# Later cycles of a coupling net computed from two products of the given state, with GpSimd's share of the work moved into the attention

## The reference, cut to what matters

```python
x = x + layernorm(attention(layernorm(x)))   # 16 heads of 8, on the left 128 features, then Wo to 256
x = x + layernorm(ffn(layernorm(x)))

def ffn(x):                                  # x: (batch, 1024, 256)
    gf = global_net(x.mean(axis=1))          # 256 -> 128 -> 64 -> 1, gelu, gelu, sigmoid
    out = x
    for _ in range(3):                       # three cycles
        tf = coupling_net(out)               # 256 -> 256 -> 128 -> 64 -> 1, three gelus, sigmoid
        coupling = 0.1 + adaptive_range * (0.7 * gf + 0.3 * tf - 0.5) * 2.0
        out = out + coupling * twist(out)
    return out

def twist(x):
    o_r, o_i, p_r, p_i = split(x, 4)
    return concatenate([p_r, -p_i, -o_r, o_i])
```

## Time and profile before

| what | value |
|---|---|
| median of 3 runs | 3441.96 us (3440.69 to 3444.75) |
| the profiled execution | 3440.79 us, span 3439.0 us |
| mean granted TensorE clock | 0.983 |
| PE / DVE / ACT / POOL busy, of the span | 96% / 86% / 84% / 28% |
| first exponential of batch 0, batch 1 | 74.4 us, 288.9 us |
| last exponentials end, span ends | 3299.4 us, 3439.0 us |

### The profile page before, as it was taken

How to read it: one execution, slowest core, us unless ns; L and a number is a source line. 1 busy time by engine, 2 the same in 40 slices (tenths; PEclk the granted TensorE clock), 3 DMA queues, 4 the chain that set the end, 5 groups by cost and what they waited for, 6 DMA issues and landing times.

```text
span 3439.0 us, 55797 instructions
## 1 busy us (share of the span) xinstructions
PE 3287.0 (96%) x19328; PEld 933.0 (27%) x19328; DVE 2964.2 (86%) x5517; ACT 2898.3 (84%) x3806; POOL 976.4 (28%) x1382
## 2 busy tenths in 40 slices
PE   6989999999999999999999999999999999999987
PEld 2222232322223232232322223232232322223222
DVE  7998989888898988989898898988989898898932
ACT  3868879798897979889798897979889798896964
POOL 5012060421406033060422406033060422404024
PEclk7998999999999999999999999999999999999998
DMA  3111111121112111111121112111111121111001
GB/s 89 26 40 43 43 38 32 43 50 42 51 32 59 33 49 44 47 45 32 42 51 42 51 32 61 32 48 45 47 45 31 43 50 42 39 32 48 7 22 37
DMA packets 97337, 144.71 MB, mean 42 GB/s; under 512 B 49312, under 2 KB 59936, under 8 KB 89248
## 3 DMA queue, kind: packets, MB, share of 16 engines
q1 hardware_dynamic: 93360, 123.83, 13.6%
q0 software_dynamic: 3696, 17.31, 2.7%
HBM read 34.61 MB, written 32.51 MB: 20 GB/s over the span
## 4 chain that ended last, share of the span: by engine, by line
PE 70%; DVE 14%; ACT 9%; issue 4%; SPq 2%; POOL 1%; DMA 1%; DVEq 0%; POOLq 0%
PE heads_ps L503 24%; PE ring_ps L470 14%; PE scoresT_ps L488 11%; DVE max_parts L949 10%; PE scoresT_ps L590 7%; ACT p_sb L700 4%; PE scoresT_ps L595 3%; DVE stats L960 2%; PE scoresT_ps L598 2%; ACT headsT L709 1%; PE scoresT_ps L601 1%; PE ring_ps L532 1%; SPq L337 1%; PE scoresT_ps L518 1%; PE heads_ps L470 1%
## 5 line engine op out<-in xcount | busy, mean ns | idle before, releaser
L949 DVE TENSOR_REDUCE max_parts<-ring_ps 128x1 f32<-128x512 f32 x3741 | 2367.9, 684 | 230.1 <-PE ring_ps L470 171.0
L700 ACT ACTIVATE p_sb<-scoresT_ps 128x1024 f32<-128x1024 f32 x2048 | 1970.9, 1025 | 82.7 <-PE scoresT_ps L488 59.1
L470 PE MATMUL ring_ps<-k_rows,q_rows 48*128 48x512 bf16 x3741 | 1079.3, 385 | 22.8 <-DVE max_parts L949 13.4
L503 PE MATMUL heads_ps<-p_sb,v_sb 128*9 128x512 f32 x8192 | 1072.5, 596 | 17.9 <-ACT headsT L709 11.9
L488 PE MATMUL scoresT_ps<-q_rows,k_rows 51*128 51x512 bf16 x4096 | 1020.6, 383 | 14.9 <-ACT p_sb L700 7.5
L470 PEld LDWEIGHTS ring_ps<-k_rows,q_rows 48*128 48x128 bf16 x3741 | 262.9, 94 | 1321.2 <-DVE max_parts L949 1210.7
L1210 POOL CAST max_wide<-max_all 128x16 bf16<-128x16 f32 x128 | 25.1, 196 | 1755.6 <-DVE max_all L955 1755.6
L590 PE MATMUL scoresT_ps<-state,w 128*128 128x512 f32 x736 | 366.6, 621 | 5.3 <-DVE state L1013 3.9
L488 PEld LDWEIGHTS scoresT_ps<-q_rows,k_rows 51*128 51x128 bf16 x4096 | 207.3, 93 | 243.3 <-ACT p_sb L700 219.9
L811 ACT ACTIVATE p_sb<-scoresT_ps,b 128x512 f32<-128x512 f32 x180 | 123.5, 686 | 167.5 <-PE scoresT_ps L590 166.6
L503 PEld LDWEIGHTS heads_ps<-p_sb,v_sb 128*9 128x9 f32 x8192 | 124.6, 89 | 288.7 <-issue 277.4
(11 more groups left out here) (206 smaller groups left out, 2767.4 us busy)
## 6 DMA issues: line engine op xcount, KB each, us to landing
q_rows<-parts SPq DMA_DIRECT2D x744, 32.0 KB
k_rows<-parts SPq DMA_DIRECT2D x744, 32.0 KB
x_sb<-in_x SPq DMA_DIRECT2D x16, 1024.0 KB, 4.9
x_in<-in_x SPq DMA_DIRECT2D x15, 1024.0 KB, 5.2
out<-x_sb SPq DMA_DIRECT2D x15, 1024.0 KB, 3.9
out<-x_in POOLq DMA_DIRECT2D x15, 1024.0 KB, 7.8
q_rows<-max_rows SPq DMA_DIRECT2D x512, 3.0 KB
feat_h<-headsT SPq DMA_DIRECT2D x512, 16.0 KB
```

The lines of the kernel that those rows point to most:

```text
L470: e.matmul(ring_bank(max_taken, u + 1), q_rows[rows, slot, pair, h * BANK + qb * P:h * BANK + (qb + 1) * P], k_rows[rows, slot, pair, kh * ...
L503: m = e.matmul(heads_ps[32 * j:32 * j + DH + 1, :], v_sb[:, b % 2, kb, 4 * (group % NG) + j, 0:DH + 1], p_sb[:, n % 2, j, :], start=(kb == ...
L700: e.activation(p_sb[:, n % 2, 2 * two:2 * two + 2, :].rearrange("p h n -> p (h n)"), scoresT_ps[:, 2 * two * BANK:(2 * two + 2) * BANK], A ...
L949: e.tensor_reduce(max_parts[:, gi % 2, kh, col:col + 1], bank_of(max_taken, u + 1), AX.X, ALU.max).then_inc(max_taken, 1)
```

## The change

Three things are done, and the beats are laid out anew (26 instead of 30 per coupling).

First, layer 1 of cycles 1 and 2 has no matmul. Cycle 0 computes u (layer 1) and v ("layer 5", the same weights with signs, on the swapped halves of the state), ACT copies both into `headsT`, which is free by then, and `mix` makes the input of the gelu from them: m = 0 on DVE, m = 1 on GpSimd, two instructions each per half c. Before the third cycle's mix, `fold` makes v - c0 u, four instructions per half c on GpSimd (in the last batch on DVE). The gelu of these reads `feat_h` and `sums_h` in SBUF.

Second, the state itself no longer stands in the way of the cycles. GpSimd makes it from the couplings of all three cycles in `spin`, six times four or more instructions per batch, in steps 5 to 20 of the next attention. The sign of the twist goes into the turned state and the weights once.

Third, the split of queries and keys is GpSimd's alone, three instructions for each of four pieces, in steps 0 to 3 of the attention; SP lays the rows from step 8 on. The first norm of batch b+2 goes from ACT to DVE (`first_norm`).

```diff
-LAYERS = ((1, 0, 0), (1, 0, 1), (2, 0, 0), (1, 1, 0), (3, 0, 0), (1, 1, 1), (4, 0, 0), (2, 1, 0), (3, 1, 0), (4, 1, 0))
-CYCLE = len(LAYERS)
-BEATS = 3 * CYCLE
+LAYERS = ((0, 1, 0, 0), (0, 1, 0, 1), (0, 5, 0, 0), (0, 2, 0, 0), (0, 5, 0, 1), (0, 3, 0, 0), (0, 1, 1, 0),
+          (0, 4, 0, 0), (0, 1, 1, 1), (0, 2, 1, 0), (0, 5, 1, 0), (0, 3, 1, 0), (0, 5, 1, 1), (0, 4, 1, 0),
+          (1, 2, 0, 0), (1, 3, 0, 0), (1, 2, 1, 0), (1, 4, 0, 0), (1, 3, 1, 0), (1, 4, 1, 0),
+          (2, 2, 0, 0), (2, 3, 0, 0), (2, 2, 1, 0), (2, 4, 0, 0), (2, 3, 1, 0), (2, 4, 1, 0))
+BEATS = len(LAYERS)
...
-BEAT_UNITS = (4, 1, 2, 1, 2, 1, 2, 2, 1, 1,
-              2, 3, 2, 3, 3, 2, 2, 4, 2, 1,
-              2, 1, 2, 3, 4, 2, 2, 2, 3, 1)
+BEAT_UNITS = (5, 6, 0, 0, 4, 0, 1, 2, 1, 3, 1, 3, 5,
+              5, 0, 2, 0, 3, 4, 3, 0, 4, 4, 2, 3, 3)
...
-STATS0, ROOT0, NORM0, TURN_X = (0, 1, 2, 3), 3, (5, 6, 7, 8), (8, 9)
-PROJECT_QK, SPLIT, PROJECT_V = (17, 18, 23, 24), (20, 21, 26, 27), (22, 29)
-BACK, STATS3, ROOT3, NORM3, ADD_OUT = (8, 9, 10, 11), (10, 11, 12, 13), 14, (16, 17, 20, 24), 26
-INVERT, DIVIDE, WO, STATS1, ROOT1 = 2, (4, 5), (5, 5, 6, 6), (6, 6, 7, 7), 7
-NORM1, ADD1, STATS2, ROOT2 = (10, 11, 12, 13), (11, 12, 13, 15), (14, 16, 17, 18), 19
-NORM2, STATE = (21, 22, 23, 24), (26, 27, 28, 29)
-GLOBAL = (0, 3, 5)
-TWIST0, UPDATE0, TWIST1, UPDATE1 = 6, 7, 9, 10
+SPLIT, SPIN = (0, 1, 2, 3), (5, 8, 11, 14, 17, 20)
+FIRST_ROW = 8
+STATS0, ROOT0, NORM0, TURN_X = (0, 0, 0, 0, 0, 2, 2, 2), 6, (4, 6, 7, 7, 7, 9, 9, 9), (7, 10)
+PROJECT_QK, PROJECT_V = (13, 14, 19, 20), (19, 23)
+BACK, STATS3, ROOT3, NORM3, ADD_OUT = (8, 9, 10, 11), (10, 10, 11, 12), 12, (13, 13, 16, 21), 25
+INVERT, DIVIDE, WO, STATS1, ROOT1 = 3, (7, 7), (7, 7, 7, 7), (7, 7, 8, 8), 8
+NORM1, ADD1, STATS2, ROOT2 = (9, 10, 11, 11), (9, 10, 11, 12), (14, 15, 16, 16), 16
+NORM2, STATE = (18, 19, 21, 21), (22, 23, 24, 25)
+GLOBAL = (1, 5, 6)
+MIX1, GELU1, FOLD, MIX2, GELU2 = (8, 13), (10, 14), (9, 15), (17, 18), (19, 20)
...
+END_SPIN, LAST_SPIN = (12, 15, 20, 20, 27, 28), (9, 15, 18, 19)
...
@@ sync_program @@
-                        for at in range(3 * n // 2, 3 * (n + 1) // 2):
+                        first, last = (96 * max(0, k - FIRST_ROW) // (STEPS - FIRST_ROW) for k in (n, n + 1))
+                        for at in range(first, last):
                             lay_row(b + 1, at)
@@ tensor_program, coupling @@
                 if layer == 1:
...
+                    e.wait_ge(state_ready, 4 * b + 2 * c + 2)
+                    e.matmul(ps, w1[:, 0, cols], state[:, b % 2, 0, half], start=True, stop=False)
+                    o = e.matmul(ps, w1[:, 1, cols], state[:, b % 2, 1, half], start=False, stop=True)
+                if layer == 5:
+                    e.matmul(ps, w1[:, 0, cols], state[:, b % 2, 1, half], start=True, stop=False)
+                    o = e.matmul(ps, w1_minus[:, cols], state[:, b % 2, 0, half], start=False, stop=True)
+                if layer == 2:
+                    e.wait_ge(activated, gelu_end(b, cycle, c, 1))
...
@@ scalar_program @@
-            def split_mid(b, i, h):
...
+                if layer in (1, 5):
+                    if m == 0:
+                        e.wait_ge(heads_laid[c], LAID * min(N, b + 2))
+                    e.activation((u_of if layer == 1 else v_of)(c, m), ps, ACT.Copy).then_inc(hid_done, 1)
...
+            def later_layer_1(b, j):
+                for cycle, places in ((1, LAST_GELU1), (2, LAST_GELU2)) if b == N - 1 else ((1, GELU1), (2, GELU2)):
+                    for c in range(2):
+                        if j == places[c]:
+                            for m in range(2):
+                                e.wait_ge(mixed[m], mix_end(b, cycle, c))
+                                e.activation(hidden[:, 0, 2 * c + m, :], turned(c, m), ACT.Gelu,
+                                             bias=b1[:, m:m + 1]).then_inc(activated, 1)
@@ vector_program @@
-            def twist(b, cycle, c):
...
-            def update(b, cycle, c):
...
+            def mix(b, cycle, c, m=0):
+                n, u, v, to = mix_end(b, cycle, c), u_of(c, m), v_of(c, m), turned(c, m)
+                by = couple_of(cycle - 1, c)
+                e.wait_ge(coupled, couple_end(b, cycle - 1, c))
+                if cycle == 1:
+                    e.wait_ge(wo_done, 4 * min(N, b + 2))
+                    e.tensor_tensor(to, by, v, ALU.mult).then_inc(mix_begun[m], 1)
+                    e.wait_ge(mix_begun[m], n)
+                    e.tensor_tensor(to, to, u, ALU.add).then_inc(mixed[m], 1)
+                else:
+                    e.wait_ge(folded, 2 * b + c + 1)
+                    e.tensor_tensor(v, by, v, ALU.mult).then_inc(mix_begun[m], 1)
+                    e.wait_ge(mix_begun[m], n)
+                    e.tensor_tensor(to, to, v, ALU.add).then_inc(mixed[m], 1)
...
+            def first_norm(b, j):
...
@@ gpsimd_program @@
+            def split(b, i, h):
+                cols, rest = slice(h * BANK, (h + 1) * BANK), proj_sb[i][h]
+                e.wait_ge(qk_evac, 4 * b + 2 * i + h + 1)
+                finished(e.tensor_tensor(rest, rest, parts[:, i, 0, cols], ALU.subtract))
+                finished(e.tensor_copy(parts[:, i, 1, cols], rest))
+                e.tensor_tensor(parts[:, i, 2, cols], rest, parts[:, i, 1, cols], ALU.subtract).then_inc(low_done, 1)
...
+            def fold(b, c):
+                by = couple_of(0, c)
+                for m in range(2):
+                    e.wait_ge(mixed[m], mix_end(b, 1, c))
+                e.tensor_tensor(u_of(c, 0), by, u_of(c, 0), ALU.mult)
+                finished(e.tensor_tensor(u_of(c, 1), by, u_of(c, 1), ALU.mult))
+                e.tensor_tensor(v_of(c, 0), v_of(c, 0), u_of(c, 0), ALU.subtract)
+                e.tensor_tensor(v_of(c, 1), v_of(c, 1), u_of(c, 1), ALU.subtract).then_inc(folded, 1)
...
+            def spin(b, cycle, c):
+                cols, by = slice(c * BANK, (c + 1) * BANK), couple_of(cycle, c)
+                real, other = state[:, b % 2, 0, cols], state[:, b % 2, 1, cols]
+                if cycle < 2:
+                    e.wait_ge(coupled, couple_end(b, cycle, c))
+                else:
+                    e.wait_ge(hid_done, end_of(b, 2, 4, c))
+                    finished(e.tensor_scalar(by, by, ar_token[:, 0:1], shift[:, 0:1], ALU.mult, ALU.add))
+                e.tensor_tensor(proj_sb[0][0], by, other, ALU.mult)
+                finished(e.tensor_tensor(proj_sb[0][1], by, real, ALU.mult))
+                e.tensor_tensor(real, real, proj_sb[0][0], ALU.add)
+                last = e.tensor_tensor(other, other, proj_sb[0][1], ALU.subtract)
...
```

More of the change, by code:

```diff
@@ new lines, in mixes @@
+            def mixes(b, j):
+                for cycle, places in mix_places(b):
+                    for c in range(2):
+                        if j == places[c]:
+                            mix(b, cycle, c)
+                        if j == LAST_FOLD[c] and cycle == 1 and b == N - 1:
+                            fold(b, c)
+            def fold(b, c):
+                by = couple_of(0, c)
+                for m in range(2):
+                    e.wait_ge(mixed[m], mix_end(b, 1, c))
+                for m in range(2):
+                    o = e.tensor_tensor(u_of(c, m), by, u_of(c, m), ALU.mult)
+                o.then_inc(last_folded, 1)
+                e.wait_ge(last_folded, c + 1)
+                for m in range(2):
+                    o = e.tensor_tensor(v_of(c, m), v_of(c, m), u_of(c, m), ALU.subtract)
+                o.then_inc(folded, 1)
@@ new lines, in mixes, with make_shift @@
+            def mixes(b, j):
+                for cycle, places in mix_places(b):
+                    for c in range(2):
+                        if j == places[c]:
+                            mix(b, cycle, c)
+                        if j == FOLD[c] and cycle == 1 and b < N - 1:
+                            fold(b, c)
+            def make_shift(b):
+                e.wait_ge(g_act, 3 * (b + 1))
+                if b:
+                    e.wait_ge(last_added, 2 * b)
+                e.tensor_scalar(shift[:, :], tg[:, :], ar_global[:, 0:1], tenth[:, 0:1], ALU.mult,
@@ L1327, in ending @@
                         make_shift(b)
[L1328 to L1333 removed]
+                    mixes(b - 1, j)
+                    mixes(b, j - SHIFT)
+                    for i in range(6):
+                        if j == END_SPIN[i]:
+                            spin(b - 1, i // 2, i % 2)
+                        if i < 4 and j == SHIFT + LAST_SPIN[i]:
+                            spin(b, i // 2, i % 2)
                     if j == ROOT3:
```

450 lines of the change are left out of this document (201 added, 249 removed).

## The result

The changed kernel takes 3491.74 us (median of 4 runs, 3487.80 to 3495.88) against 3441.32 us before beside it: ratio 1.0149, interval 1.0127 to 1.0170. It is 50 us slower; I had forecast 12 us faster. The profiled execution took 3487.8 us.

A forecast was written before the change was run, and what follows sets the result against it. ScalarE bounds the attention and TensorE the coupling stage, where GpSimd's chain would take over. Stages -13, start -2, batch 0 and attentions 0, ending +2 sum to -13: 3428, as a median 3429 us; range 3375 to 3465.

The forecast's parts named there:

- SP lays the 96 row pieces in 56 steps instead of 64 ... Cost 0: Attention: SyncE issues the pieces at 0.7 us each, long before step 48 needs the first; cost 0.
- the cover of a late cut: Attention: a lead of 112 products covers cuts of the maxima delayed by spins; 75 us if it failed.
- "+2" for the ending: Ending: GpSimd's order delays the mixes, the last coupling is 4 us shorter; sum +2 us, between -4 and +8.
- The stage's walk: Coupling stage, step by step: first GpSimd bias at 20.7 us, last layer 3 done at 70.7 against 71.6 before.
- The 0.9 us gained per stage: Coupling stages 1 to 14: the last layer 3 ends 0.9 us earlier in each, 13 us in 14.
- GpSimd becomes the bound: Coupling stage: GpSimd runs without a pause from first bias to mix 2, so TensorE's saving mostly becomes idle time.
- "-2" for the start: Start: ScalarE's conversions ahead of the first exponential go; -2 us, between 0 and -3.
- GpSimd's chain ends later: Rival, coupling stage: collisions put mix 2 of half 0 at 62.1; +2.2 us per stage, about 3478; chance 0.25.
- The clock drops: Rival, coupling stages: TensorE's waits lower its clock; 6 us of each at half clock gives 3471; chance 0.03.
- the signs of being wrong: TensorE without waits for GpSimd, attention maxima over 0.60 us apart, or granted clock under 1.00 in stages 1 to 14.
- batch 0's stage: Coupling stage of batch 0: more VectorE work against ScalarE and GpSimd work removed; 0, between -4 and +3 us.
- GpSimd's list stretches: Coupling stage: collisions with VectorE's two-input instructions lengthen GpSimd's list by 2.4 us, bounds 0 and 4.0.

The follow-up runs named there:

- a1: The changed kernel with its 96 row pieces laid from step 3 of the attention instead of step 8; 3462.67 us (1.0059).
- a3: The changed kernel with the spins in the attentions cut to one of 512 columns; 3490.04 us (1.0138).
- b1: a1 with the folds cut to one of 512 columns for batches before the second-last; 3456.33 us (1.0037).
- c1: a1 with the output projection's bias added by VectorE instead of ScalarE and GpSimd, and another ending; 3459.76 us (1.0051).
- d1: c1 with start and ending reordered: root 3 before all spins, spins behind norm 2, those of half 1 on VectorE; 3438.50 us (0.9987).
- e1: d1 with four first normalisations moved to beat 4 and the last batch's spins shared by GpSimd and VectorE; 3434.47 us (0.9977).

## Why the prediction was wrong

- **"SP lays the 96 row pieces in 56 steps instead of 64 ... Cost 0"** is the step that failed. The term was 0. The attentions grew by 27.3 us, and rows from step 3 (a1) take back 18.4 of it and 8 in the stages, 29 us in the medians: that is what the late rows cost, nearly half of the 63 us that the forecast missed. The walk checked when the first piece is needed, not how much the queue has to issue: pieces, heads, maxima's rows and transposes fill it from 2385 to the attention's end. The prediction named the cover of a late cut (75 us if it failed) and looked at GpSimd for the cause, where a3 shows none.
- **"+2" for the ending** was mis-sized: +18.3. Its place was right (mixes behind folds, spins and roots on GpSimd), but I let GpSimd's lateness reach TensorE only through the mixes, not through ScalarE's normalisation in front of a GELU nor through VectorE's stretched passes. The first coupling grew by 16.3 us (0 to 4 forecast). The last one was forecast 4 us shorter and came 1.9 longer: from 3408.71 to the second half of the final turn at 3474.14 it is 65.4 us, and 63.5 in the earlier trace rows.
- **The stage's walk was right, its reading not.** Measured in the stage behind attention 11, from TensorE's first layer 1 (2502.09): first bias at 20.5 (20.7 forecast), last layer 3 done at 70.7 (70.7 forecast). The 0.9 us gained per stage came where the clock held (75.8 to 76.1 for 76.9); the other ten took 77.0 on average, and the sum moved by -0.5 for -13. With SyncE out of the way (a1) the stages fell 8.4 us in sum. Yet "GpSimd becomes the bound" is wrong for GpSimd alone: b1 takes 10 us off its list for 0.1 us, and the rows put the end of VectorE's list 0.7 us from GpSimd's. I gave VectorE 62 us of work and room; it had 65.3, and c1, which takes out its waits for GpSimd's sums and 5 us of GpSimd's list at once, gains 1.1 us a stage.
- **"-2" for the start**: +2.4. In a1 TensorE waits 3.15 and 1.36 us for the first normalisations, which VectorE now makes between maxima; d1, with them ahead and batch 0's products closer together, starts 1.5 us earlier than c1. I had costed them as work (2 us) and not as places in its order.
- The rivals: "GpSimd's chain ends later" came nearest (3478) for a wrong reason: mix 2 of half 0 ended at 58.2 in the stage behind attention 11, where that rival has 62.1 and the forecast 59.0. "The clock drops" had 0.03, with the reason that no wait in the walk was over 2 us; a granted clock under 1.00 in stages 1 to 14, one of the signs of being wrong, came in ten of them. Part of the 8.9 to 15.5 us that the attentions keep in a1 to e1 is the first steps of some of them at a lower clock too. In d1, us 1928 to 1933, the start of attention 9:

```profile
1928.00:1933.00 5.00, 4.37 (x20) 0.69 (x21) 3.75 (x7) 3.79 (x5) 4.49 (x5) 0.71 0.63 211
```

These attentions take 130.9 us, the others 129.3; before, nearly all took 129.0. In a1, c1, d1 and e1 each of them came behind a stage in which the clock had already fallen once, but not every such stage was followed by one; what sets it was not settled. Nor were the 0.3 us of the others, which the spins do not make: attentions 3 and 14 of a3 took 129.3 too.

- Right: TensorE's work per stage fell and became idle time; the spins in the attention are free; batch 0's stage; that GpSimd's list stretches where VectorE's two-input instructions and GpSimd's meet, though it was less (1.3 us up to mix 2 of half 0 behind attention 11, 2.4 taken).

By the Trainium skill ("SBUF — State Buffer", who interferes with whom) a tensor_scalar in a two-port mode and GpSimd lock each other out; the rows of 2.62 us beside a spin and 0.72 without agree, and here that rule had a price: 7.5 us in one pass of eight against the pace of the pairs.
